# Product keys: sums kept in two banks each, pairs of heads added on GpSimd before the turning on TensorE

## The reference

```python
xn = _rmsnorm(x, norm_w)
q = (xn @ w_q.T).reshape(b, t, H, 2, DK)                      # H = 8 heads
sim1 = jnp.einsum('bthd,hkd->bthk', q[..., 0, :], keys[:, :, 0, :])   # 32 keys
sim2 = jnp.einsum('bthd,hkd->bthk', q[..., 1, :], keys[:, :, 1, :])
s1, i1 = jax.lax.top_k(sim1, K); s2, i2 = jax.lax.top_k(sim2, K)      # K = 8
all_sc = (s1[..., :, None] + s2[..., None, :]).reshape(b, t, H, K * K)
fs, pk = jax.lax.top_k(all_sc, K)                             # the 8 best of 64 sums
fi = jnp.take_along_axis(all_idx, pk, axis=-1)                # which of 32 x 32 experts
hidden = jax.nn.gelu(jnp.einsum('btd,bthkd->bthk', xn, expert_down[fi]), approximate=False)
hidden = hidden * jax.nn.relu(fs)
return jnp.einsum('bthk,bthkd->btd', hidden, expert_up[fi])
```

## Time and profile before

| what | value |
| --- | --- |
| median of 3 runs | 2434.55 us (2427.18 to 2437.85) |
| profiled execution, its own time | 2428.99 us |
| its span | 2427.1 us |
| PE busy | 1968.5 us (81%) |
| DVE busy | 1660.0 us (68%) |
| ACT busy | 1069.3 us (44%) |
| POOL busy | 535.3 us (22%) |
| thresholds of the product keys stage | 256 of 1277 ns, from 1157.0 to 1776.0 us |
| turning matmuls of the stage | 2048 of 274 ns |

### The profile page before, as it was taken

One profiled execution on the slowest core, in us unless ns is written; L12 is line 12 of the kernel. 1 busy time (PEld: TensorE's weight loads), 2 busy tenths in 40 slices (PEclk: granted clock), 3 DMA queues, 4 the chain that ended last, 5 costly groups with the idle time before them and its releaser, 6 DMA issues. The chain is left out here.

```text
span 2427.1 us, 32168 instructions
## 1 busy us (share of the span) xinstructions
PE 1968.5 (81%) x10146; PEld 1277.5 (53%) x10146; DVE 1660.0 (68%) x3948; ACT 1069.3 (44%) x2364; POOL 535.3 (22%) x610
## 2 busy tenths in 40 slices
PE   8999799856699992324999999999867997986697
PEld 5666544334477661212666766766635454444444
DVE  4555378856223226885999898988843697997567
ACT  3433355433243430002665666665511575655344
POOL 1222044422000001211000000000000377777111
PEclk9999899966799995666999999999986998997788
DMA  2000000031000003100000000000040022222010
GB/s 79 26 26 18 26 18 18 17 113 43 35 27 26 17 0 90 35 9 26 1 5 14 1 5 14 6 1 6 5 181 8 26 58 63 60 68 62 31 52 26
DMA packets 39095, 81.45 MB, mean 34 GB/s; under 512 B 9030, under 2 KB 20622, under 8 KB 38214
## 3 DMA queue, kind: packets, MB, share of 16 engines
q1 hardware_dynamic: 30790, 63.25, 7.7%
q0 software_dynamic: 8192, 16.79, 2.6%
HBM read 63.24 MB, written 16.78 MB: 33 GB/s over the span
## 5 line engine op out<-in xcount | busy, mean ns | idle before, releaser
L1866 ACT ACTIVATE pk_sums<-pk_sum 128x512 f32<-128x512 f32 x448 | 243.1, 595 | 228.7 <-PE pk_sum L2092 217.6
L1968 DVE SCALAR_TENSOR_TENSOR pk_level<-pk_sums,pk_least 128x1024 f32<-128x1024 f32 x256 | 324.1, 1277 | 23.8 <-ACT pk_sums L1866 22.7
L2099 PE MATMUL pk_weights<-product_keys_early_ident,pk_level 128*128 128x128 f32 x2048 | 268.1, 274 | 35.9 <-DVE pk_level L1968 35.9
L2309 POOL DMA_INDIRECT tk_values<-top_keys_values,tk_index x256 | 243.3, 950 | 199.7 <-DVE tk_index L2475 123.1
L2099 PEld LDWEIGHTS pk_weights<-product_keys_early_ident,pk_level 128*128 128x128 f32 x2048 | 232.6, 141 | 102.1 <-issue 66.6
L2624 PE MATMUL tk_to_act<-tk_keys,tk_xT 128*128 128x512 f32 x512 | 237.8, 617 | 31.0 <-ACT tk_scores L2375 30.4
L2624 PEld LDWEIGHTS tk_to_act<-tk_keys,tk_xT 128*128 128x128 f32 x512 | 98.4, 198 | 152.7 <-issue 97.9
L2091 PE MATMUL pk_sum<-pk_lay_rows,pk_partsT 96*128 96x512 bf16 x448 | 170.2, 380 | 0.2 <-ACT pk_sums L1866 0.2
L2092 PE MATMUL pk_sum<-pk_lay_columns,pk_partsT 96*128 96x512 bf16 x448 | 169.3, 378 | 0.0
L1381 PEld LDWEIGHTS moe_outs<-experts_early_w,moe_hT 128*128 128x128 f32 x1024 | 133.9, 193 | 62.1 <-issue 62.0
L1316 DVE SCALAR_TENSOR_TENSOR moe_r<-moe_outs,moe_gates,moe_r 128x128 f32<-128x128 f32 x128 | 36.0, 344 | 173.2 <-PE moe_outs L1381 173.2
(11 more groups left out here) (398 smaller groups left out, 3818.8 us busy)
## 6 DMA issues: line engine op xcount, KB each, us to landing
moe_x<-x_after_attention SPq DMA_DIRECT2D x8, 512.0 KB, 3.6
tk_scores<-top_keys_compress SPq DMA_DIRECT2D x1, 4096.0 KB, 15.5
tk_values<-top_keys_values,tk_index POOLq DMA_INDIRECT x256, 2.5
att_x_proj<-x_first SPq DMA_DIRECT2D x4, 512.0 KB, 5.1
att_x_res<-x_first SPq DMA_DIRECT2D x4, 512.0 KB, 4.3
x_after_attention<-att_y SPq DMA_DIRECT2D x4, 512.0 KB, 4.8
x_after_experts<-moe_y SPq DMA_DIRECT2D x8, 256.0 KB, 2.0
lin_x<-x_after_experts SPq DMA_DIRECT2D x4, 512.0 KB, 4.2
```

The costliest lines, as they stand in the source:

```text
L1866: act.activation(sums[:, n % SUMS, half * HALF:(half + 1) * HALF], bank[:], ACT.Copy).then_inc(S.free.sem, 1)
L1968: dve.scalar_tensor_tensor(level[:, n % LEVELS, :], sums[:, n % SUMS, :], least[:, t % 2, h:h + 1], sums[:, n % SUMS, :], ALU.is_ge, ALU.m ...
L2099: ins = pe.matmul(weights[:, ch * P:(ch + 1) * P], level[:, n % LEVELS, ch * P:(ch + 1) * P], ident[:], is_transpose=True, start=h == 0 an ...
L2309: pool.indirect_dma_start(out=values[:, slot, k, :], out_offset=None, in_=c["values"], in_offset=bass.IndirectOffsetOnAxis(ap=index[slot][ ...
```

## The change

Five things are changed together, in the product keys stage alone.

1. PSUM: the three banks for halves of sums and `to_dve` are gone; there are two tiles `sum_banks` of 1024 columns (two banks each), one head each. `build_sum(n)` builds a whole head and waits for `level_ready` of head n-2, that is, for its threshold. ACT copies a head in one instruction.
2. All eight heads are built on PE; `shift` is gone. `transpose_parts` turns 8 instead of 7 combinations a time.
3. `keep` reads the sum twice, once in PSUM and once as ACT's copy in SBUF.
4. Two heads at a time share a `level` buffer. POOL adds the second to the first (`merge`), and PE turns the pair once (`add_levels`), one pair behind the heads: the turning of pair q-1 stands behind the build at odd heads. The weighing stands behind `keep` of head 2, no longer ahead of head 0's.
5. `rest_of` and `low_of` go from DVE to POOL. The up product takes a bank of `to_act`, stands at head 3, and ACT copies it to `added_up`; `finish` reads that, and comes at head 5 rather than 2.

```diff
-    ON_TENSOR = [h for h in range(HEADS) if h not in on_vector]
-    PER_FILL = len(ON_TENSOR)
+    COMBOS = 2 * HEADS
+    PER_FILL = COMBOS // 2
     AHEAD = 2
-    SUMS = 4
-    LEVELS = 4
+    PAIRS = HEADS // 2
+    KEPT_PAIRS = 3
+    SUMS = 3
...
-        sum_banks = [m.psum(f"sum{i}", [P, HALF]) for i in range(3)]
+        sum_banks = [m.psum(f"sum{i}", [P, E]) for i in range(AHEAD)]
         weights = m.psum("weights", [P, CHUNKS * P])
-        to_dve = m.psum("to_dve", [P, HALF])
...
+            def merge(q):
+                own = level[:, q % KEPT_PAIRS]
+                pool.wait_ge(level_ready, 2 * (q + 1))
+                pool.tensor_tensor(own[:, 0, :], own[:, 0, :], own[:, 1, :], ALU.add).then_inc(merged, 1)
...
+            def take_sum(n):
+                act.wait_ge(sum_full, n + 1)
                 after(act, level_ready, n - SUMS + 1)
+                act.activation(sums[:, n % SUMS, :], sum_banks[n % AHEAD][:], ACT.Copy).then_inc(sum_ready, 1)
+            def take_up(t):
...
+                act.activation(added_up[:, g % 2, i, :], bank[:, 0:P], ACT.Copy).then_inc(A.free.sem, 1)
...
             def keep(t, h):
                 n = t * HEADS + h
-                if h in ON_TENSOR:
-                    dve.wait_ge(S.free.sem, taken_from_S(BUILT.index((t, h))))
-                after(dve, summed, n - LEVELS + 1)
-                dve.scalar_tensor_tensor(level[:, n % LEVELS, :], sums[:, n % SUMS, :], least[:, t % 2, h:h + 1],
+                dve.wait_ge(sum_ready, n + 1)
+                if n % 2 == 0:
+                    after(dve, summed, n // 2 - KEPT_PAIRS + 1)
+                dve.scalar_tensor_tensor(level[:, n // 2 % KEPT_PAIRS, n % 2, :], sum_banks[n % AHEAD][:], least[:, t % 2, h:h + 1],
                                          sums[:, n % SUMS, :], ALU.is_ge, ALU.mult).then_inc(level_ready, 1)
...
+            def build_sum(n):
+                t, h = divmod(n, HEADS)
+                pe.wait_ge(A.free.sem, taken_from_A("partsT", t, h * 2 // PER_FILL))
+                after(pe, level_ready, n - AHEAD + 1)
                 for half in range(2):
...
+            def add_levels(q):
+                pe.wait_ge(merged, q + 1)
...
+                    n = t * HEADS + h
+                    build_sum(n + AHEAD)
+                    if h == 2:
+                        project_down(beside[1:2])
+                    if h % 2 == 1:
+                        add_levels(n // 2 - 1)
+                    if h == 3 and t > 0:
+                        project_up(t - 1)
                     if chained:
                         if h == 5:
                             transpose_parts(t + 2, 0)
                         if h == 7:
                             transpose_parts(t + 2, 1)
```

More of the change, by code:

```diff
@@ L1855, in gelus @@
                     act.activation(gelu[:, g % 2, ch, :], bank[:], ACT.Gelu).then_inc(A.free.sem, 1)
-            def take_sum(unit):
-                if unit is None:
+            def take_sum(n):
+                if n >= UNITS:
                     return
-                t, h = unit
-                n = t * HEADS + h
+                act.wait_ge(sum_full, n + 1)
                 after(act, level_ready, n - SUMS + 1)
-                for half in range(2):
-                    act.wait_ge(S.full.sem, S.to_take(0))
-                    bank = S.take()
-                    act.activation(sums[:, n % SUMS, half * HALF:(half + 1) * HALF], bank[:], ACT.Copy).then_inc(S.free.sem, 1)
+                act.activation(sums[:, n % SUMS, :], sum_banks[n % AHEAD][:], ACT.Copy).then_inc(sum_ready, 1)
+            def take_up(t):
+                g, i = divmod(t, PER_HALF)
+                act.wait_ge(A.full.sem, A.to_take(0))
+                if i == 0:
+                    after(act, r_ready, g - 1)
+                bank = A.take()
+                act.activation(added_up[:, g % 2, i, :], bank[:, 0:P], ACT.Copy).then_inc(A.free.sem, 1)
             squares(0)
@@ L1992, in _ @@
             norm_x(0)
-            for t in range(2):
-                rest_of(t)
-                low_of(t)
             tops_of(0, range(HEADS))
@@ new lines, in build_sum @@
+                    pe.matmul(bank, partsT[:, t % 3, 2 * h, :], lay_rows[:, half * HALF:(half + 1) * HALF], start=True, stop=False)
+                    ins = pe.matmul(bank, partsT[:, t % 3, 2 * h + 1, :], lay_columns[:], start=False, stop=True)
+                ins.then_inc(sum_full, 1)
+            def add_levels(q):
+                if q < 0:
+                    return
+                t, p = divmod(q, PAIRS)
+                if p == 0:
+                    after(pe, weighed_ready, t)
+                pe.wait_ge(merged, q + 1)
@@ L2122, in _ @@
                 transpose_parts(t, 1)
-            for unit in BUILT[0:AHEAD]:
-                build_sum(unit)
+            for n in range(AHEAD):
+                build_sum(n)
             for t in range(ALL):
```

154 lines of the change are left out of this document (65 added, 89 removed).

## The result

The changed kernel takes 2489.74 us (median of 4 runs, 2486.47 to 2491.72) against 2430.86 (4 runs on the same chip): a ratio of 1.0238, 95% interval 1.0207 to 1.0269. Slower, as forecast, but by 2.4% instead of 1.2%. The profiled run has 2490.15 us and a span of 2488.2, which is 61.1 more than before.

A forecast was written before the change was run, and what follows sets the result against it. PE came first, DVE close behind, and added bank waits were to outweigh PE's saved work. Terms 15+6+3+3+5+4+2-2 gave +36 us on the profiled 2428.99, so 2465, own range 2445 to 2490.

The forecast's parts named there:

- rival (3): Clock falls behind PE's idle gaps in plain tiles: 2500 us if every second tile, 2527 if every tile; chance 0.21.
- the walk through the plain tile: Queues followed from one keep(7) to the next, ending at 20.02, taken as 19.9 against 19.35: +0.55 us per tile, +15.
- `keep` at 1.28 beside the merges: DVE's threshold, first operand now in PSUM, keeps its old 1.28 us beside POOL's merges.
- Merges at 2.35: POOL's four merges per tile priced at 2.35 us each beside DVE; above 2.6 would mean unpriced contention.
- `pairs` at nothing: DVE's `pairs_of` (0.68) can wait 0 to 2.35 us for POOL; costed at nothing, covered by the up product.
- my terms for `finish`, squares, transposes, norm and last tiles: Extras in odd tiles: `finish` +6, squares +5, x transposes +4, norm +2, last three tiles -2 us.
- none of my gaps is as long as 2.65: Argument against a clock fall: PE's predicted idle places are 0.6 to 1.4 us per tile.
- `finish` +0.85, seven times: DVE's `finish`, every fourth tile, waits for a running merge: -0.3 to +1.6 us, taken as +0.85, +6 in all.
- three such operations: DVE operations left with both inputs in SBUF, open to POOL contention: `pairs_of`, the floor, and `finish` every fourth tile.
- Rival (1), the work sets the pace, 17.45 us a tile,: PE does 15.7 us, its waits stay as they are: -61, with end terms +16, 2384 us; chance 0.22.

The follow-up runs named there:

- e2: Changed kernel with first down product and x transposes (and their ACT copies) queued behind head 2's sum: ratio 1.0101 to the kernel before, plain tile 18.74 us.
- e9: Changed kernel with only the up product cut in halves, four chunks ahead of head 6's sum and four behind: ratio 1.0187 to the kernel before.
- e3: Changed kernel with `keep` reading both operands from ACT's copy in SBUF, waits and order untouched: ratio 1.0697 to the kernel before.
- e1: Changed kernel with POOL's merge narrowed from 1024 to 8 columns, leaving odd heads out of the result: ratio 1.0169 to the kernel before.
- e10: Changed kernel with queues reordered, up product in halves, odd work spread over ScalarE and GpSimd, next tile's floor on GpSimd: ratio 0.9751 to the kernel before.
- e11: e10 with ScalarE's four normalising operations at heads 4 to 7 instead of 2 to 5: ratio 0.9745 to the kernel before.
- e7: e2 plus later squares, residual add and normalising on GpSimd, score behind head 2's sum, up product in halves: ratio 1.0087 to the kernel before.
- e8: Changed kernel without GpSimd's merges, TensorE turning both heads of each pair, eight turnings a tile: ratio 1.0342 to the kernel before.

## Why the prediction was right in sign and half in size

The sign was right for the reason given; the size was not. By its own sum the change was to cost 36 us on the profiled execution, and it cost 61. By the medians it is 30 against 59, since the sum was added to an execution 5.6 us below the median that it was then compared with. That 2489.74 still lies inside the forecast's own range, 2445 to 2490, by 0.3 us, is luck: the walk through the plain tile gives 13 of the 61 us, and much of the rest came from falls of the clock, which the forecast had left to rival (3) with its 2500.

**The plain tile: right.** Forecast 19.9 by a walk that ended at 20.02; measured 19.78, so +0.44 instead of +0.55, and 13 us instead of 15. Its places came within 0.3 us each: down product 3.8 (measured 3.69 after keep(7)'s end), sum of head 2 at 4.66 (4.63), keep(2) at 6.86 (6.75), sum of head 6 at 14.95 (14.77), keep(6) at 17.15 (16.89). That these are causes is shown by moving them: e2 takes the down product out (-1.04), e9 half the up product (-0.64).

**`keep` at 1.28 beside the merges: right.** 1277 ns, and e3 shows the price of the alternative. **Merges at 2.35: nearly.** Their mean is 2464 because one in four is 2.82, where `pairs` runs at its start; it cost nothing, since PE waited 3.4 us in all for them. **`pairs` at nothing: right,** although it doubled: keep(4) and keep(5) had their sums, and the up product covered them, as the price said.

**The odd tiles: this step failed.** Before, they held 5 us over plain ones; my terms for `finish`, squares, transposes, norm and last tiles added 15, together 20. Measured: 53. The 21 tiles split as follows: `finish` tiles 4 x 2.25 = 9; the seven tiles behind a `finish` 14; squares 11; norm 5; `finish` with transposes 3 x 4.37 = 13; the last 1.

The term that I had put at nothing is the clock. I turned it away as rival (3), since "none of my gaps is as long as 2.65". Those were the gaps of a plain tile. I had not walked PE's queue through the odd tiles, where `finish`, the squares and the norm make gaps of 2.59, 2.29 and 1.79 us. By the tile from 1691.53 on, the falls are the whole of what six of the seven tiles behind a `finish` hold over plain ones, 10 us; the seventh, with 4, lies where the last tiles begin and was not separated. In the squares tiles they are about 6 of the 11 us, an estimate: 22.51, 23.79 and 23.75 us stand against 21.29 at a clock of 1.00 in e1, where the same tile takes 23.62 at 0.86. What is left of the squares is 1.5 us each, as forecast. So of the 33 us that I missed the clock took at least 16.

The term "`finish` +0.85, seven times" was too small as well, but by little. At full clock the `finish` tile and the one behind it take 2.25 us more than two plain ones, against 0.90 before: +1.34, inside the bounds of -0.3 to +1.6. This is the add, at 2.04 instead of 0.67. I counted "three such operations" left for contention by their number of SBUF inputs, and so left out the tensor_scalar operations with one SBUF tensor: the normalising, 3.14 instead of 1.10, which cost nothing here, and the norm of the next x (389 instead of 282 ns in the mean). e1 shows that contention with the merges, with the gaps and the falls of the clock that follow from it, is 32 of the 53 us, and the 21 left are what I had forecast for all of it. In e10 and e11, where all of this is spread over ScalarE and GpSimd, no odd tile is more than 1.7 us over a plain one, but for e10's long one (2.9).

The Trainium skill, SBUF — State Buffer, "Who interferes with whom", also says that `tensor_scalar` can enter a two-port mode and then contends with GpSimd, the later one standing still for the whole instruction. The trace agrees (0.17 against 2.27 us in e7). I had weighed the same section's rule on two inputs and passed over this one.

**Rival (3), the clock, was half right.** Its sign came: a clock of 0.94 over the 30 tiles, where under 0.97 was to speak for it. It was to fall behind gaps in plain tiles; it fell in odd tiles and the tiles behind them only, and made them up to 2.2 us longer (the tile behind `finish` is 19.78 at 1.00 and 21.94 at 0.84). The gaps ahead of the falls come from contention (`finish`, norm) and from ScalarE's queue (squares), as e1 shows. In e8, with PE busy 90%, and in e11, with DVE's long stretches gone, the 30 tiles run at 0.99 to 1.00. How much of the 47 us is clock in the norm tiles, in `finish` with transposes and in the last ones was not separated. **Rival (1), the work sets the pace, 17.45 us a tile,** did not happen in this order, but it is what the change can give in another order, with the floor moved to GpSimd too: e11's plain tile is 16.82 with PE busy 16.13, 2.5 less than before.

## What to carry to other kernels

When a buffer is freed by its last reader instead of by a copy, walk the queue of the engine that refills it: everything ahead of the refill is now on the path (one product of 0.86 us, moved behind the refill, gave back 1.04 us a tile). When an idle engine is given long operations, list every operation that they slow on its neighbour (here GpSimd's on VectorE), the tiny ones and the rare ones too, and price each at the remainder of the long one: merging was worth 17 us where such operations were left beside it, and 73 where they were gone. Then walk the rare tiles through every queue as you walked the plain one, and look for the longest gap of PE: at 12 of 13 such gaps the clock fell here, and the tile behind paid up to 2.2 us for it.

## What the runs showed of the hardware

- DVE beside a 128x1024 GpSimd add: unchanged are scalar_tensor_tensor and tensor_tensor of 128x1024 with one PSUM and one SBUF input (1279 and 1214 ns, against 1273 and 1216 elsewhere in the changed kernel's trace) and MAX8 of 128x32 (177 ns in e7 either way). Longer are tensor_tensor with two SBUF inputs (670 to 2043), scalar_tensor_tensor with two (1272 to 2570 in e3), and tensor_scalar from SBUF to SBUF (336 to 845 in the mean of all; 0.17 to 2.27 us in e7). GpSimd's add itself takes 2.82 instead of 2.35 us where `pairs` runs at its start.
- The granted clock fell to half (1.2 GHz) at 12 of 13 PE gaps of 1.79 to 2.59 us in a stage where PE was busy 82%, as in the earlier trace rows behind one of 2.65. At the same gap of 2.59 us it fell in one tile (21.94 us) and not in another (19.78 us).
- Four normalising operations of 128x128 take GpSimd 3.1 us, DVE 1.1 alone, and ScalarE 1.65 as activations with scale and bias.
